# A graph layer on one core: block-first tile space, near blocks loaded up to four bands at a time, and row finishing moved from GpSimd to VectorE

## The chip, the cores and the metric

The kernel runs on one core of a Trainium2 chip, as one launch. The metric is device time in microseconds (us); the kernel before takes 1089.55 us (median of 3 runs, 1089.52 to 1090.64). Lower is better.

## The reference

`x` is 8192 x 128 and `adj` is 8192 x 8192, all float32. `adj` is 256 MiB, so reading it is the bulk of the traffic.

```python
def _L0_gnn_ref(x, adj, w):
    A = adj + jnp.eye(adj.shape[0], dtype=adj.dtype)
    deg = jnp.sum(A, axis=1)
    d_isqrt = jax.lax.rsqrt(deg)
    A_hat = A * d_isqrt[:, None] * d_isqrt[None, :]
    h = jnp.matmul(A_hat, x)
    return jax.nn.elu(jnp.matmul(h, w))
x = _layernorm(x + _L0_gnn_ref(x, adj, L0_gnn_w), axis=-1)
```

Row sums of `adj` are needed before any product that uses them: the product of a column band t of `A` with band t of `x` needs the square root of the degrees of row band t.

## The kernel before, in words

The 8192 rows and columns are cut into 16 bands of 512. Tile (t, u) is the 512 x 512 piece of `adj` in row band u and column band t, 1 MiB. SBUF holds 22 slots of 1 MiB (`SLOTS`), each either a tile or a "home", which is band t of `x` scaled by d and copied four times over quadrants for TensorE. Steps for a tile: a load on SyncE's queue; row sums on ScalarE (ACT) by a copy with `accum_out`, one instruction for each block of 128 rows; a transposition of 32 x 32 blocks on VectorE (DVE), called a turn; then a TensorE (PE) step of 64 matmuls against home t, which handles one to four tiles at once; then DVE adds the product from PSUM into `hT`. In the code a step is a "part", and a "job" is what is summed in one of the two PSUM sets (`SETS`) before one add.

A home t can be made only when row band t has been read completely, since only then is its degree known. Therefore rows are read ahead: of row t the tiles that can't be kept are read for their sums alone ("far" loads, up to 2048 columns wide) and read a second time late ("again"), and those near the diagonal are kept ("first"). The last load of row t is the diagonal tile (t, t). On it follow, in this order, ACT's sum, DVE's reduction of the sums (`deg`), on GpSimd (POOL) the addition of the identity to the diagonal tile and then the power -1/2, on DVE the scaling of `x` (line 803) and ten of the sixteen copies into the home (line 810), the other six on ACT (line 668). PE's first step on home t needs these.

When all 16 products of row band u are added, the row is finished: an "out" on PE (four matmuls with `w`), then z on ACT (scale by d, line 686), two Relu and an Exp on ACT, ELU on DVE (828), residual on POOL (639), statistics on DVE (836, 842), deviation on POOL (645, 649), shift on DVE (849), normalisation (702) and store on ACT.

The order of each engine's instructions is fixed ahead by `plan()`, a planner in Python that plays the work through with assumed durations, and the engines then run these lists with semaphores between them. Nothing is reordered while the kernel runs. `KEEP` says how many tiles may be kept over which bands, `FEED` how many loaded tiles may wait before rows are read on, `FLIGHT` how many loads the planner holds in flight, `MERGE` how many tiles one step takes. Tiles merge into one step only if their slots lie at equal distances of less than 16 (`even_slots`).

## Time and profile before

| | |
|---|---|
| median of 3 runs | 1089.55 us |
| the profiled execution | 1089.98 us |
| its span, first to last instruction | 1087.7 us |
| mean granted TensorE clock | 0.956 of full speed |
| PE busy | 929.3 us (85%) |
| DVE busy | 807.2 us (74%) |
| ACT busy | 809.3 us (74%) |
| POOL busy | 78.7 us (7%) |
| bytes moved by DMA | 363.89 MB |

The profiled execution took 2.3 us more than its span. Durations below are from it. Busy shares are averages over stages with different limits, so the rows further down are taken stage by stage. DMA queues run behind their issue: a load is issued some 13.4 us (median) before it lands.

### The profile page before, as it was taken

The numbers are of one execution on the slowest core, as the hardware profiler recorded it, in microseconds if no ns is written. First come the engines' busy times: TensorE is split into PE (matmuls) and PEld (weight loads), VectorE is DVE, ScalarE is ACT, GpSimd is POOL, SyncE is SP. The second block draws the span as 40 slices with busy tenths as digits, with TensorE's granted clock in tenths as the row PEclk, the third lists the DMA queues.
The fourth block names the chain that finished last, engine by engine and source line by source line (L and its number), as shares of the span: only waits on it lengthen the run. The fifth ranks groups of instructions, "written<-read, shape, count | busy, mean of one in ns | idle before, by whom it ended". The sixth has DMA issues, their size and how long they took to land.

```text
span 1087.7 us, 36085 instructions
## 1 busy us (share of the span) xinstructions
PE 929.3 (85%) x16128; PEld 831.2 (76%) x16128; DVE 807.2 (74%) x761; ACT 809.3 (74%) x2033; POOL 78.7 (7%) x87
## 2 busy tenths in 40 slices
PE   0089399399698988999999999999997999999993
PEld 0077289297475755998889999999896889899993
DVE  0686686694868697998789999999975765757822
ACT  6898898898899999898999999967419756200203
POOL 0000000000000000000000000010101130100101
PEclk9999799699698998999999999999998999999997
DMA  9999999999999999999999999958984979799910
GB/s 379 383 391 409 385 393 408 383 388 403 385 398 390 396 383 394 386 395 376 395 396 378 369 375 320 320 192 266 306 293 150 324 215 315 250 325 309 366 72 20
DMA packets 178506, 363.89 MB, mean 335 GB/s; under 512 B 6192, under 2 KB 34480, under 8 KB 170672
## 3 DMA queue, kind: packets, MB, share of 16 engines
q1 hardware_dynamic: 161456, 353.20, 89.4%
q10 hardware_dynamic: 16896, 8.39, 2.6%
q8 instruction: 127, 2.08, 0.8%
q14 instruction: 27, 0.22, 0.1%
HBM read 357.37 MB, written 4.19 MB: 332 GB/s over the span
## 4 chain that ended last, share of the span: by engine, by line
PE 38%; issue 24%; DMA 21%; ACT 5%; DVE 4%; SPq 4%; POOL 3%; POOLq 0%; DVEq 0%
PE p_set L772 38%; DMA tile<-in_adj 20%; ACT tile L660 4%; SPq L611 4%; DVE tile L810 2%; POOL tile L639 1%; POOL rstd L649 1%; DVE hT L821 1%; DMA xn<-in_x 1%; DVE tile L790 1%; POOL tile L628 1%; DVE xn L803 0%; POOL var_eps L645 0%; ACT tile L668 0%; PE p_set L746 0%
## 5 line engine op out<-in xcount | busy, mean ns | idle before, releaser
L772 PE MATMUL p_set<-tile 32*128 32x256 f32 (+3 forms) x16000 | 912.5, 386 | 138.6 <-DVE tile L790 59.5
L772 PEld LDWEIGHTS p_set<-tile 32*128 32x128 f32 x16000 | 815.7, 189 | 231.2 <-issue 141.9
L790 DVE STREAM_TRANSPOSE tile<-tile 128x2048 f32<-128x2048 f32 x256 | 583.5, 2297 | 161.4 <-ACT tile L660 92.2
L660 ACT ACTIVATE tile<-tile 128x512 f32<-128x512 f32 (+2 forms) x824 | 592.6, 720 | 49.4 <-DMA tile<-in_adj 44.6
L668 ACT ACTIVATE tile<-xn 32x512 f32<-32x512 f32 x208 | 130.4, 627 | 31.6 <-DVE xn L803 24.1
L660 ACT ACTIVATION_READ_ACCUMULATOR tile<-tile 128x1 f32 x824 | 153.9, 187 | 0.0
L821 DVE TENSOR_TENSOR hT<-p_set,hT 128x512 f32<-128x512 f32 (+1 forms) x137 | 109.0, 828 | 55.2 <-PE p_set L772 54.5
L686 ACT ACTIVATE tile<-p_set,d 128x128 f32<-128x128 f32 x64 | 18.2, 366 | 158.2 <-PE p_set L746 158.2
L810 DVE COPY tile<-xn 32x512 f32<-32x512 f32 x160 | 66.8, 418 | 5.0
L628 POOL TENSOR_TENSOR tile<-tile,ident 128x512 f32<-128x512 f32 x16 | 20.4, 1274 | 686.4 <-ACT tile L660 686.4
L702 ACT ACTIVATE tile<-tile,shift,rstd 128x128 f32<-128x128 f32 x64 | 26.1, 485 | 29.1 <-DVE shift L849 29.1
L639 POOL TENSOR_TENSOR tile<-tile 128x512 f32<-128x512 f32 x16 | 20.3, 1268 | 267.9 <-DVE tile L828 267.9
L803 DVE TENSOR_TENSOR xn<-xn,d 128x512 f32<-128x512 f32 x23 | 15.2, 660 | 11.8 <-DMA xn<-in_x 11.8
L746 PEld LDWEIGHTS p_set<-w_sb,hT 128*128 128x128 f32 x128 | 15.5, 191 | 10.5 <-issue 6.1
L823 DVE COPY hT<-p_set 128x1024 f32<-128x1024 f32 (+1 forms) x7 | 9.6, 1372 | 18.7 <-PE p_set L772 18.7
L746 PE MATMUL p_set<-w_sb,hT 128*128 128x128 f32 x128 | 18.5, 287 | 5.3 <-DVE hT L821 4.1
L828 DVE SCALAR_TENSOR_TENSOR tile<-tile 128x512 f32<-128x512 f32 x16 | 10.7, 669 | 8.4 <-ACT tile L696 8.4
L649 POOL TENSOR_TENSOR rstd<-var_eps,half 128x4 f32<-128x4 f32 x16 | 16.6, 1037 | 1.3
L634 POOL TENSOR_TENSOR d<-deg,half 128x4 f32<-128x4 f32 x16 | 16.3, 1020 | 4.5 <-DVE deg L796 4.3
L836 DVE BATCH_NORM_STATS2 stats<-tile 128x6 f32<-128x128 f32 x64 | 13.5, 273 | 1.6 <-POOL tile L639 1.6
L695 ACT ACTIVATE tile<-tile 128x512 f32<-128x512 f32 x16 | 10.1, 630 | 0.5
L693 ACT ACTIVATE tile<-tile 128x512 f32<-128x512 f32 x16 | 10.1, 630 | 0.4
(15 smaller groups left out, 30.8 us busy)
## 6 DMA issues: line engine op xcount, KB each, us to landing
tile<-in_adj SPq DMA_DIRECT2D x331, 1024.0 KB, 13.4
xn<-in_x SPq DMA_DIRECT2D x23, 256.0 KB, 12.0
tile<-in_x ACTq DMA_DIRECT2D x16, 256.0 KB, 7.7
out_rows<-tile ACTq DMA_DIRECT2D x16, 256.0 KB, 8.3
w_sb<-in_w SPq DMA_DIRECT2D x1, 64.0 KB, 1.9
```

Source lines behind the costliest of these rows:

```text
L611: sp.dma_start(shaped(k), source(loads[k])).then_inc(loaded[slot_of[k]], 16)
L628: nc.gpsimd.tensor_tensor(on_diagonal, on_diagonal, ident[:, :].unsqueeze(1).to_broadcast([128, BLOCKS, 128]), ALU.add)\
L639: nc.gpsimd.tensor_tensor(pos[:, n % RING], pos[:, n % RING], res[:, n % RING], ALU.add).then_inc(y_ready, 1)
L649: nc.gpsimd.tensor_tensor(rstd[:, n % RING], var_eps[:, :], half[:, :], ALU.pow).then_inc(rstd_ready, 1)
L660: ins = nc.scalar.activation(view[:, g], view[:, g], ACT.Copy, accum_out=to[:, g:g + 1])
L668: nc.scalar.activation(xs_part(h, q, s), xn[quadrant(s), h % XN], ACT.Copy).then_inc(copied_by["act"], 1)
L702: ins = nc.scalar.activation(pos[:, n % RING, b], pos[:, n % RING, b], ACT.Identity, bias=shift[:, n % RING, b:b + 1], scale=rstd[:, n % R ...
L746: ins = nc.tensor.matmul(p[:, 0, F * b:F * (b + 1)], hT[:, at:at + 128], w_sb[:, :], start=True, stop=True)
L772: ins = nc.tensor.matmul(to, xs_of(h)[quadrant(q), j], moving, start=first and s == b == 0, stop=last and s == b == 3)
L790: nc.vector.transpose(tiles[slot_of[k]], tiles[slot_of[k]]).then_inc(tile_turned, 1)
L810: nc.vector.tensor_copy(xs_part(h, q, s), xn[quadrant(s), h % XN]).then_inc(copied_by["dve"], 1)
L821: nc.vector.tensor_tensor(rows, new, rows, ALU.add).then_inc(product_added, 1)
```

## The change

The space of 22 slots is laid out with the block index first: `[128, BLOCKS, SLOTS, BAND]` instead of `[128, SLOTS, 2048]`. A tile is now four runs of 512 columns, 22 x 512 apart, and slots n and n+1 lie side by side in each block. So any two tiles may form one step, and one load can bring 2 or 4 neighbouring bands of a row: `near` loads of 4 bands x 1 block (8 KB rows) or 2 bands x 2 blocks (4 KB rows) in place of 4 or 2 tile loads with 2 KB rows. Far loads now have a ring of their own, four rows of 1 MiB in slots 0 to 3, which become ordinary slots when the last far load is summed. Constants of the planner change, and its rules (a step of m tiles isn't taken if it would leave one over). The home's copies come in three pieces, and the planner calls a home usable after the first. The diagonal addition is held back until the power if the diagonal tile completes the row. z, the positive part plus residual, ELU, statistics and the sum of variance and epsilon are on DVE; ACT keeps one Relu and the Exp, POOL the power alone.

Over the whole program the planner's lists hold these numbers, before and now: steps of 1, 2, 3, 4 tiles 11, 99, 13, 2 and 4, 112, 8, 1 (125 steps both); adjacency loads 331 and 336 (331 and 333 MiB, since 77 tiles are read again, not 75); of these `near` loads none and 30 (8 of four bands, 22 of two); row sums on ACT 824 and 744 instructions; homes 23 and 22.

```diff
-KEEP = (12, 9, 10)
+STAGE = 4
+KEEP = (12, 11, 7)
-STAY = 13
+STAY = 12
+WIDTHS = (4, 2)
-FEED = 10
-FLIGHT = 4
+FEED = 12
+FLIGHT = 5
+FIRST_COPIES = [("dve", [(0, q) for q in range(Q)]), ("act", [(2, 2), (2, 3)] + [(3, q) for q in range(Q)]),
+                ("dve", [(1, q) for q in range(Q)] + [(2, 0), (2, 1)])]
+LATE_COPIES = [("act", [(s, q) for q in range(Q)]) for s in range(Q)]
...
+    def near_loads():
+        left = [v for v in row_todo if v[0] == "near"]
+        r, slots = left[0][2], sorted(n for _, n in free)
+        for w in WIDTHS:
+            if len(left) < w or len(free) < w + 1 or left[0][1] - left[w - 1][1] != w - 1:
+                continue
+            runs = [n for n in slots if all(n + i in slots for i in range(w))]
+            if not runs:
+                continue
+            base, t0, nk = runs[0], left[w - 1][1], BLOCKS // w
...
+            return [("near", r, nk * j, nk, t0, w, base, j, group) for j in range(w)]
+        _, t, r = row_todo.pop(0)
+        return [tile_load("first", t, r)]
...
+    def tile_summed(i):
+        _, t, u, _, _ = tiles[i]
+        if t != u:
+            offer("dve", 4 if t in known else 6, "turn", i, 2.35)
+        elif sums_left[u]:
+            offer("pool", 1, "diagonal", i, 1.4)
+        else:
+            held_diagonals[u] = i
...
         elif kind == "power":
             known.add(arg)
             offer("dve", 0, "scale", home_of[arg], 0.7)
+            if arg in held_diagonals:
+                offer("pool", 1, "diagonal", held_diagonals.pop(arg), 1.4)
...
-        tile = sb("tile", [128, SLOTS, 2048])
-        tiles = [tile[:, n] for n in range(SLOTS)]
+        space = sb("space", [128, BLOCKS, SLOTS, BAND])
+        slots = [space[:, :, n] for n in range(SLOTS)]
...
+            if load[0] == "near":
+                _, _, k0, nk, _, w, base, _, _ = load
+                return space[:, k0:k0 + nk, base:base + w].rearrange("p k n c -> p k (n c)")
+            _, _, _, nk, _, wide, row = load
+            return space[:, row, 0:STAGE].rearrange("p n c -> p (n c)")[:, 0:nk * wide].rearrange("p (k c) -> p k c", k=nk)
...
-                k = arg
-                wait_vacant(sp, ("load", k))
-                sp.dma_start(shaped(k), source(loads[k])).then_inc(loaded[slot_of[k]], 16)
+                load = loads[arg]
+                if load[0] == "tile":
+                    wait_vacant(sp, ("tile", load[5]))
+                elif load[0] == "near" and not load[7]:
+                    for i in near_groups[load[8]]:
+                        wait_vacant(sp, ("tile", i))
+                elif load[0] == "far" and row_before[arg] is not None:
+                    sp.wait_ge(act_summed, sum_nth[row_before[arg]])
+                sp.dma_start(home_of(load), source(load)).then_inc(arrival(arg), 16)
...
-                            moving = bass.AP(chunk.tensor, chunk.offset, [[SLOTS * 2048, 32], [2048 * step, len(at)], [BAND, BLOCKS], [1, 32]])
+                            moving = bass.AP(chunk.tensor, chunk.offset, [[BLOCKS * SLOTS * BAND, 32], [BAND * step, len(at)], [SLOTS * BAND, BLOCKS], [1, 32]])
...
+                elif kind == "z":
...
+                    nc.vector.tensor_tensor(pos[:, n % RING], p_set[set_of_out[n]][:, 0, :].rearrange("p (b f) -> p b f", b=BLOCKS),
+                                            d[:, finals[n]].unsqueeze(2).to_broadcast([128, BLOCKS, F]), ALU.mult).then_inc(z_ready, 1)
+                elif kind == "relu":
...
+                    nc.vector.scalar_tensor_tensor(out=res[:, n % RING], in0=pos[:, n % RING], scalar=0.0, in1=res[:, n % RING],
+                                                   op0=ALU.max, op1=ALU.add).then_inc(relu_added, 1)
                 elif kind == "elu":
...
+                    nc.vector.scalar_tensor_tensor(out=pos[:, n % RING], in0=neg[:, n % RING], scalar=-1.0, in1=res[:, n % RING],
+                                                   op0=ALU.add, op1=ALU.add).then_inc(y_ready, 1)
...
+                    nc.vector.tensor_scalar(var_eps[:, n % RING], mv[:, n % RING, :, 1], EPS, None, ALU.add).then_inc(var_ready, 1)
```

VectorE, at the point where row band 8 has been read completely (`TENSOR_REDUCE deg` is its degree, line 803 or 889 the scaling, line 810 or 896 the copies into home 8, 821 or 907 adds from PSUM). Before:

```order
L790 STREAM_TRANSPOSE tile<-tile 128x2048
L796 TENSOR_REDUCE deg<-sums 128x4
L790 STREAM_TRANSPOSE tile<-tile 128x2048
L803 TENSOR_TENSOR xn<-xn,d 128x512
L810 COPY tile<-xn 32x4x128 x10
L821 TENSOR_TENSOR hT<-p_set,hT 128x4x4x32 x3
L790 STREAM_TRANSPOSE tile<-tile 128x2048 x2
L821 TENSOR_TENSOR hT<-p_set,hT 128x4x8x32
```

and now:

```order
L876 STREAM_TRANSPOSE space<-space 128x4x512
L882 TENSOR_REDUCE deg<-sums 128x4
L889 TENSOR_TENSOR xn<-xn,d 128x512
L896 COPY space<-xn 32x4x128 x10
L907 TENSOR_TENSOR hT<-p_set,hT 128x4x8x32
L876 STREAM_TRANSPOSE space<-space 128x4x512
L907 TENSOR_TENSOR hT<-p_set,hT 128x4x8x32
L876 STREAM_TRANSPOSE space<-space 128x4x512 x2
```

The turn of the diagonal tile, which stood between the degree and the scaling, now stands behind the copies. The three adds behind the copies, which free both PSUM sets, have become one; the other set's add now stands ahead of the degree.

TensorE, in the late stage, on the last seven steps of the group of rows 4 and 5 (a step is x64; 128x256 is a step of two tiles, 128x128 of one; `w_sb` is an out). Before:

```order
L746 MATMUL p_set<-w_sb,hT 128x128 x4
L772 MATMUL p_set<-tile 128x256 x64
L746 MATMUL p_set<-w_sb,hT 128x128 x4
L772 MATMUL p_set<-tile 128x128 x128
L772 MATMUL p_set<-tile 128x256 x192
L772 MATMUL p_set<-tile 128x128 x128
```

and now:

```order
L858 MATMUL p_set<-space 128x256 x64
L836 MATMUL p_set<-w_sb,hT 128x128 x4
L858 MATMUL p_set<-space 128x256 x64
L836 MATMUL p_set<-w_sb,hT 128x128 x4
L858 MATMUL p_set<-space 128x256 x256
L858 MATMUL p_set<-space 128x128 x128
```

The first pair of single tiles has become one step of two; the second pair, which uses two different homes, is still two steps.

SyncE's list of loads, from its beginning (128x4x512 is a tile, 128x2048 a far load or, now, also a load of four bands). Before:

```order
L611 DMA tile<-in_adj 128x2x1024 x2
L611 DMA tile<-in_adj 128x2048 x8
L611 DMA tile<-in_adj 128x4x512 x6
L607 DMA xn<-in_x 128x4x128
L611 DMA tile<-in_adj 128x4x512 x9
```

and now:

```order
L723 DMA space<-in_adj 128x2x1024 x2
L723 DMA space<-in_adj 128x2048 x12
L723 DMA space<-in_adj 128x2x1024 x2
L713 DMA xn<-in_x 128x4x128
L723 DMA space<-in_adj 128x4x512 x11
```

Of the twelve loads of 2048 columns eight are far and four bring bands 2 to 5; the two behind them bring bands 0 and 1. The load of `x` stands behind the same 16 MiB.

## Rows read from the trace of the kernel before

**Rows 1.** Windows: length; busy PE, PEld, DVE, ACT, POOL; PE clock; DMA share; GB/s
```profile
59.50:598.80 539.30, 470.21 (x7812) 398.54 (x7812) 422.99 (x338) 498.54 (x1291) 20.32 (x18) 0.93 1.04 392
598.80:1068.20 469.40, 456.74 (x8304) 430.65 (x8304) 355.32 (x382) 254.78 (x623) 50.05 (x54) 0.99 0.83 276
...
740.00:830.00 90.00, 83.31 (x1480) 77.84 (x1476) 72.05 (x81) 47.15 (x93) 10.48 (x12) 0.96 0.81 264
...
1068.20:1087.70 19.50, 2.30 (x18) 1.94 (x16) 6.38 (x21) 9.02 (x22) 5.37 (x6) 0.65 0.09 27
```
**Rows 2.** Waits from 100 to 600 us: total us, times, longest
```profile
PE p_set L772 <- DVE tile L810: 57.6, 5, 18.7
```
**Rows 3.** Timeline around the last load of row 8: start us, length us
```profile
547.04 0.63 ACT L660 ACTIVATE tile<-tile 128x512 f32<-128x512 f32 x1
...
550.72 0.18 DVE L796 TENSOR_REDUCE deg<-sums 128x4 f32<-128x68 f32 x1
550.99 2.31 DVE L790 STREAM_TRANSPOSE tile<-tile 128x2048 f32<-128x2048 f32 x1
553.23 0.65 DVE L803 TENSOR_TENSOR xn<-xn,d 128x512 f32<-128x512 f32 x1
553.91 4.45 DVE L810 COPY tile<-xn 32x512 f32<-32x512 f32 x10
558.39 1.89 DVE L821 TENSOR_TENSOR hT<-p_set,hT 128x512 f32<-128x512 f32 x3
...
559.74 2.64 PE L772 MATMUL p_set<-tile 32*128 32x256 f32 x41 [2.70 <-DVE hT L821]
```
**Rows 4.** The same around the last load of row 7
```profile
504.04 0.63 ACT L660 ACTIVATE tile<-tile 128x512 f32<-128x512 f32 x1
...
507.91 1.01 POOL L634 TENSOR_TENSOR d<-deg,half 128x4 f32<-128x4 f32 x1
...
512.81 2.54 PE L772 MATMUL p_set<-tile 32*128 32x256 f32 x32 [2.28 <-DVE tile L810]
```
**Rows 5.** Windows with far loads alone, and with tile loads
```profile
9.00:31.00 22.00, 0.00 (x0) 0.00 (x0) 0.00 (x0) 18.79 (x22) 0.00 (x0) 1.00 1.01 416
56.00:85.00 29.00, 25.55 (x420) 23.87 (x424) 25.52 (x15) 28.58 (x85) 0.00 (x0) 1.00 1.05 390
```
**Rows 6.** PE's timeline: steps of two tiles, then of one tile
```profile
783.50 21.00 PE L772 MATMUL p_set<-tile 32*128 32x256 f32 x384
...
882.63 4.97 PE L772 MATMUL p_set<-tile 32*128 32x128 f32 x168
890.02 6.31 PE L772 MATMUL p_set<-tile 32*128 32x128 f32 x128 [2.42 <-issue]
```
**Rows 7.** Timeline of the end, after the last step
```profile
1068.28 1.22 DVE L821 TENSOR_TENSOR hT<-p_set,hT 128x1024 f32<-128x1024 f32 x1 [26.24 <-PE p_set L772]
...
1079.02 1.26 POOL L639 TENSOR_TENSOR tile<-tile 128x512 f32<-128x512 f32 x1
...
1083.27 1.65 ACT L702 ACTIVATE tile<-tile,shift,rstd 128x128 f32<-128x128 f32 x4 [1.28 <-DVE shift L849]
```
**Rows 8.** Groups by form: count, busy us, mean ns
```profile
L821 DVE TENSOR_TENSOR hT<-p_set,hT 128x512 f32<-128x512 f32 x102 | 64.6, 673 | 21.8 <-PE p_set L772 21.6
L772 PE MATMUL p_set<-tile 32*128 32x128 f32 x1408 | 43.5, 277 | 2.7 <-issue 2.7
```
**Rows 9.** PE's waits for adds from 598.8 to 1068.2 us
```profile
PE p_set L772 <- DVE hT L821: 6.1, 4, 3.2
...
PE p_set L746 <- DVE hT L821: 2.6, 1, 2.6
```
**Rows 10.** Timeline: far loads summed one after the other by ACT
```profile
16.28 1.91 ACT L660 ACTIVATE tile<-tile 128x2048 f32<-128x2048 f32 x1 [0.48 <-DMA tile<-in_adj]
...
18.77 1.91 ACT L660 ACTIVATE tile<-tile 128x2048 f32<-128x2048 f32 x1 [0.49 <-DMA tile<-in_adj]
```
**Rows 11.** The page's part 6, DMA issues: KB each, us to landing
```profile
tile<-in_adj SPq DMA_DIRECT2D x331, 1024.0 KB, 13.4
...
w_sb<-in_w SPq DMA_DIRECT2D x1, 64.0 KB, 1.9
```

More of the change, by code:

```diff
@@ L111, in allowed @@
         if kind == "out":
-            return free_set() is not None and len(late) == LATE and counts["outs"] == counts["z"]
+            return free_set() is not None and counts["residuals"] > 0 and counts["outs"] == counts["z"]
         if kind == "z":
@@ new lines, in next_load @@
+        if pick_row:
+            pick_row = bool(free_rows) if row_todo[0][0] == "far" else len(free) >= 2
+        if firsts and free and (backlog < FEED or not pick_row):
+            t, u = firsts.pop(0)
+            return tile_load("first", t, u)
+        if pick_row:
+            if row_todo[0][0] == "far":
+                row = min(free_rows)
+                free_rows.remove(row)
+                return row_todo.pop(0) + (row[1],)
+            queued.extend(near_loads())
+            return queued.pop(0)
@@ L409, in plan @@
     assert len(finals) == BANDS and counts["stored"] == BANDS
-    return loads, slot_of, homes, tenants, late, jobs, parts, finals, order, turns, (now, busy, dma)
+    return loads, tiles, homes, tenants, late, jobs, parts, finals, order, turns, (now, busy, dma)
 def gcn_resnorm(nc: bass.Bass, x: bass.AP, adj: bass.AP, w: bass.AP, out: bass.AP):
@@ L417, in gcn_resnorm @@
     AX = mybir.AxisListType
-    loads, slot_of, homes, tenants, late, jobs, parts, finals, order, turns, _ = plan()
+    loads, tiles, homes, tenants, late, jobs, parts, finals, order, turns, _ = plan()
     def nth_of(engine, kind):
@@ new lines, in signal_of @@
+    def signal_of(load):
+        if load[0] == "far":
+            return ("row", load[6])
+        return ("slot", load[4]) if load[0] == "tile" else ("slot", load[6] + load[7])
+    near_groups = {}
+    for i, (_, _, _, _, some) in enumerate(tiles):
+        if loads[some[0]][0] == "near":
+            near_groups.setdefault(loads[some[0]][8], []).append(i)
+    arrived, counts = [], {}
+    for load in loads:
+        counts[signal_of(load)] = counts.get(signal_of(load), 0) + 16
+        arrived.append(counts[signal_of(load)])
@@ new lines, in arrival, with sums_of, xs_chunk @@
+        def arrival(k):
+            kind, n = signal_of(loads[k])
+            return (row_loaded if kind == "row" else loaded)[n]
+        def sums_of(load):
+            if load[0] == "tile":
+                _, _, t, u, _, _ = load
+                return sums[:, BLOCKS * u:BLOCKS * (u + 1), t]
+            _, r, k0, nk, at, _ = load[:6]
+            return sums[:, BLOCKS * r + k0:BLOCKS * r + k0 + nk, at // BAND if load[0] == "far" else at]
+        def xs_chunk(h, j):
+            return slots[homes[h][1]][:, j // Q, F * (j % Q):F * (j % Q + 1)]
@@ L579, in wait_vacant @@
                 engine.wait_ge(part_out, last_part[arg] + 1)
-            elif loads[arg][0] == "far":
-                engine.wait_ge(act_summed, sum_nth[arg])
+            elif what == "stage":
+                engine.wait_ge(act_summed, max(sum_nth[k] for k in row_before))
             else:
@@ L748, in _ @@
                     continue
-                job, h, ks, first, last = parts[arg]
+                job, h, these, first, last = parts[arg]
                 bank, rows, _ = jobs[job]
```

484 lines of the change are left out of this document (246 added, 238 removed).

## The prediction

> **What bounds the kernel now.** I read the windows first. The profiled execution has three parts [rows 1]. From 59.5 to 598.8 us the DMA share is full (1.04, 392 GB/s) and PE is busy only 470.2 of 539.3 us: reading bounds. From 598.8 to 1068.2 us PE is busy 456.7 of 469.4 us at a clock of 0.99 while DMA has fallen to 276 GB/s: PE bounds. The last 19.5 us are a chain for the two last rows. DVE and ACT are busier than 70% on the whole, but neither is the limit in either stage.
>
> Next the waits tell what PE lacks in the first stage: 57.6 us in 5 waits for copies into a home [rows 2]. A home needs the degree of its row band, and this needs the last load of the row. So the first stage is a chain of restarts, one for each band: last load of row t lands, ACT sums it, DVE and POOL make d, DVE scales and copies, PE starts. Then PE has a fixed stock of work, since each band opens the same tiles whatever the planner does. I counted this in both lists of loads: row 7 ends after 185.75 MiB, row 8 after 202.00 and row 9 after 216.25, before and now, and when PE begins with bands 7, 8 and 9 it has 148, 136 and 125 of the 256 tiles left, before and now. Only the last restart before PE is full counts; a gain at an earlier one is waited away at the next. The last two with idle time worth naming are at 512.8 us (band 7, 2.28 us waited) and 559.7 (band 8, 2.70 waited) [rows 3, 4]. After that PE waits 8.7 us for adds and hardly at all for anything else [rows 1, 9].
>
> **Part 1: loads of two and four bands.** Far loads with 8 KB rows ran at 416 GB/s, tile loads with 2 KB rows at 390 [rows 5]: 2.52 against 2.69 us for a MiB, 0.17 us less. Up to the end of row 8 the new order brings 8 MiB in loads of four bands (8 x 0.17 = 1.4 us) and 14 MiB in loads of two, with 4 KB rows that no row here prices; between 0 and 0.17 I take the middle (14 x 0.085 = 1.2 us). Term: -2.6 us, from 0 to -3.7. All of it is on the path while reading bounds.
>
> The Trainium skill speaks against this term: "DMA: Bandwidth & Descriptors", section Specifications, asks for transfers of at least 512 B for line rate, so rows of 2 KB would run as fast as rows of 8 KB. By this rule the term would be 0 and the sum 2.6 us higher. The trace does not agree, by its 416 against 390 GB/s.
>
> **Part 2: the way from a row's last load to PE's first step.** At band 8 it took 559.74 - 547.04 = 12.7 us [rows 3]: ACT's sum (four times the 0.63), the degree at 550.72 (behind a turn), the turn of the diagonal tile until 553.2, scaling 0.65, ten copies 4.45, then adds from 558.39, of which the first two must free a PSUM set before PE may start. In the new list the diagonal turn stands behind the copies, and the add that frees the set stands ahead of the degree. What is left: degree done at 550.9, power 1.01 [rows 4], scaling 0.65, four of ten copies 1.8, some 0.2 for hand-overs: 554.6. That is only when the home is ready; PE must also have finished band 7. There the diagonal turn is replaced by another turn between degree and scaling, so only the copies shorten: power done at 508.9, turn until 509.2, scaling and four copies 2.45, so PE starts at 511.8 in place of 512.8. Its twelve tiles are now six steps of two, 21.00 / 3 = 7.0 us each [rows 6], with 1 us for a first step that catches up with the copies: 511.8 + 43 = 554.8. So band 8 starts at 554.8, not 559.7. Term: -4.9 us, from 0 (other work on DVE gets in between) to -6. It adds to part 1, since both move the restart. What is late next is nothing until band 9: 11 tiles are five steps of 7.0 and one of 43.5 / 11 = 3.95 [rows 8], 38.95 us, before 39.1.
>
> **Part 3: fewer single tiles in the PE-bound stage.** Two single tiles in a row cost more than a step of two: from 882.63 to 890.02 + 6.31 = 896.33 there are 296 records, 40 of them of the next step (40/128 x 7.0 = 2.2 us), so two singles took 11.5 us [rows 6]. They are one step of 7.0 now. Term: -4.5 us. The second such pair stays, one more single is gone for a triple (under 1 us, from 0). Steps of three and four in place of two I price at 0: they have the same columns to stream, and those in question are few (13 and 2 before, 8 and 1 now).
>
> **Part 4: the end.** Before, POOL's residual of the last row, 1.26 us, stands in the chain at 1079.02, late by the first row's work on POOL [rows 7], and so do a second Relu of ACT and z in four instructions. New chain from 1068.28: add to 1069.5, out to 1070.8, z on DVE priced as the add of 512 columns, 0.67 [rows 8], then the second out 71.6 to 72.7 and z to 73.5; the first row's ELU and statistics hold DVE until 75.7, the second row's (Relu and residual and ELU at 0.67 each, estimated 1.5 for statistics and variance) until 78.5; power 79.6, shift 79.8, and ACT's normalisation waits for the first row's until 80.4, so 82.1. Before, normalisation ended at 1083.27 + 1.65 = 1084.9. One more store issue of 0.4 stands behind it. Term: -2.4 us, from 0 to -4.
>
> **Part 5: what is added.** z, Relu with residual and the variance sum put about 0.67 + 0.67 + 0.2 us on DVE for each of 16 rows, 25 us in all, nearly all in the PE-bound stage, where DVE is busy 355 of 469 us [rows 1]. z stands on DVE behind PE's out, and an engine that waits there holds back all turns behind it. In this stage PE waits 6.1 and 2.6 us for adds [rows 9] and only 12.7 us in all (469.4 - 456.7, rows 1), so hardly for a turn: the turns have a lead that covers this; if the cover is gone, PE pays up to the DVE time of the dense part, 7 rows x 1.54 = 11 us. A PSUM set is now freed by DVE in its turn, and behind a turn of 2.3 us; the new list again has a single-set collision behind the rows 8 and 9. Term: +1.5 us, from -1 to +11. ACT loses 80 sum instructions and POOL its row work; neither is on the path, so 0. The two further MiB of reading fall in the late stage (DMA share 0.83), so 0. Block-first turns, copies and matmul operands have the same element counts; strides are larger, and no row shows that case. I take 0, because the old home copies already wrote four pieces 2 KB apart and took 4.45 / 10 = 0.45 us each; with 256 turns a 1% slower turn would be 6 us of DVE and only partly on the path.
>
> **Sum.** 1089.98 - 2.6 - 4.9 - 4.5 - 2.4 + 1.5 = 1077.1 us against the profiled execution, 2.3 of it outside the span. That execution was 0.4 us above the median of the runs, so 1076.7; I say 1077.
>
> **The rivals.**
>
> *The ring of far loads starves the queue (slower).* SyncE may issue a far load only when the one four before it has been summed, and everything behind it waits too, tile loads and `x` included. Loads land every 2.49 us there [rows 10], so four take 10.0 us; the sum needs 1.9 and a little more, the transfer 2.5, and issue to landing of a small load takes 1.9 [rows 11]: some 3.5 us are left for ACT to be late. ACT is busy 498.5 of 539.3 us in this stage [rows 1], and its six copies into a home come in one piece. Against it: the queue is deep (13.4 us from issue to landing, rows 11), and tile loads between far loads stretch the ring. Some 62 far loads to the end of row 8 reuse a row; from 12.9 / 62 = 0.2 us lost at each, the whole gain is gone. At 0.4 us each it is 25 us: 1077 + 25 = 1102. Chance 0.08.
>
> *DVE becomes the bound where rows are finished.* From 740 to 830 us DVE is busy 72.05 of 90 us [rows 1]; seven rows add 11, which is 92%, before any wait for PE's outs. For it: waits in program order. Against it: rows 9. It gives back about 8 us: 1085. Chance 0.17.
>
> *Reading is not earlier.* Groups of two or four bands need adjacent slots that are all vacated, their tiles are turned only when every load of the group is summed, and 18 slots serve tiles where 22 did. Parts 1 and 2 then come to nothing: 1077 + 7.5 = 1084. The row at 550.72, late by a turn, speaks for it, since the new lists have turns there too. Chance 0.13.
>
> *More than forecast.* With shorter idle times the clock stays up (0.93 in the first stage, rows 1), and the 8.7 us that PE waits for adds in the second [rows 9] go too: 1077 - 8 = 1069. Chance 0.15.
>
> **How the numbers follow.** The forecast has 0.47, the ring 0.08, DVE 0.17, reading 0.13, more 0.15. The bounds of the terms, joined, go from about 1067 to 1088; this also takes in the DVE and reading cases and half of the last. It leaves out the ring and the other half of the last, 0.15 together. The likeliest case alone is 1072 to 1081. A measurement can't tell less than 0.2% from no change, 2.2 us: faster is below 1087.4. The forecast, the better case and nearly all of DVE and reading are there: 0.88. Same 0.04, from the ends of these two. Slower 0.08, the ring.
>
> **What would show it.** Part 1: over 395 GB/s up to the start of band 8. Part 2: not over 8.5 us from the landing of row 8's last load to the first step of band 8, and PE's long full stretch begins at 590 to 593 us, where 125 tiles are left. Part 3: only three steps of 128 columns behind it, and 462 to 467 us from there to the last step. Part 4: 17 us from the last step to the end. Part 5: no wait of PE for turns in the late stage, and z rows of about 0.67 us. The forecast is wrong if DMA falls below 385 GB/s in the first stage (ring), if PE waits for line 876 after 740 us (DVE), or if turns take over 2.35 us each.

## The result and the profile after

The changed kernel takes 1085.2 us (median of 5 runs, 1083.96 to 1086.72) against 1089.55 before (now of 5 runs, 1088.8 to 1091.97); the ratio is 0.9951, with a 95% interval of 0.9931 to 0.9972. It is faster, by some 4 to 5 us where 12.5 were forecast. The time is inside the range of 1067 to 1088, above the likeliest case's own 1072 to 1081. The profiled execution took 1086.72 us, its span 1084.9.

I cut the span of after where I cut it before [rows 1]: at the step with 125 tiles left and at the end of the last step. Two windows are added for what follows.

```profile
core 0: us, PE busy (x) PEld busy (x) DVE busy (x) ACT busy (x) POOL busy (x), PEclk, DMA share, GB/s
59.50:599.70 540.20, 469.81 (x8066) 434.58 (x8066) 428.14 (x307) 486.00 (x1203) 20.45 (x18) 0.94 1.02 386
599.70:1068.10 468.40, 457.15 (x8048) 415.12 (x8048) 376.44 (x418) 221.96 (x492) 27.71 (x26) 0.99 0.85 285
1068.10:1084.90 16.80, 2.33 (x20) 1.94 (x16) 8.27 (x27) 5.70 (x12) 2.39 (x2) 0.67 0.11 31
910.00:1062.00 152.00, 143.60 (x2572) 132.34 (x2568) 104.86 (x93) 23.22 (x43) 4.03 (x4) 0.99 0.82 275
340.00:600.00 260.00, 240.08 (x4228) 228.01 (x4232) 219.78 (x168) 233.37 (x600) 12.84 (x12) 0.96 1.00 374
```

The last two windows in the kernel before:

```profile
340.00:600.00 260.00, 240.78 (x4040) 200.77 (x4036) 221.28 (x191) 243.39 (x649) 13.60 (x12) 0.97 1.04 389
910.00:1062.00 152.00, 150.14 (x2830) 141.06 (x2826) 96.75 (x80) 25.71 (x57) 10.13 (x12) 1.00 0.81 274
```

The stage that reading bounds is not shorter but 0.9 us longer, and from 340 to 600 us it reads at 374 in place of 389 GB/s with a DMA share of 1.00 in place of 1.04. And PE, which before was busy 150.1 of 152 us near the end, is busy 143.6. Both losses are in stretches where the forecast had a gain or nothing. The stations below are worked out from the traces of the profiled executions (us; "125 left" and "40 left" are the starts of the first step with so many tiles to go; row 8 and 9 are the landings of these rows' last loads):

```
                                 row 8   row 9   125 left  40 left  last step ends  span
before                           547.0   586.1   598.8     922.5    1068.2          1087.7
after                            548.5   591.0   599.7     913.8    1068.1          1084.9
slots given back (e1)            546.9   590.2   598.3     914.7    1058.5          1075.8
before, slots kept back (e2)     546.7   585.9   600.3     925.1    1077.6          1097.1
no near loads (e3)               551.2   592.5   603.6     921.8    1076.3          1093.2
rows as before (e4)              548.9   590.4   598.8     915.5    1067.4          1087.0
after, half products (e5)        540.5   578.4   587.4     878.7    1008.0          1024.7
before, half products (e6)       544.4   582.9   595.6     878.0     997.5          1017.0
e1, restart undone (e7)          565.6   612.5   625.3     954.3    1098.9          1115.6
e1, five steps split (e8)        549.3   589.8   598.3     932.8    1076.4          1093.1
before, restart as after (e9)    546.6   585.8   595.3     925.1    1072.8          1092.3
e1, other constants (e10)        547.8   586.5   595.1     904.3    1049.2          1065.5
```

So after against before: +0.9 to 125 left, -9.6 from there to 40 left, +8.6 over the last 40 tiles (154.3 in place of 145.7), -2.7 behind the last step: -2.8 us of span.

Who waits in the first stage: SyncE's waits from 340 to 640 us, first of after, then of before (total, times, longest).

```profile
SPq L723 <- PE p_set L858: 152.3, 34, 9.3
SPq L691 <- PE p_set L858: 19.0, 3, 6.5
SPq L723 <- ACT space L764: 6.0, 6, 3.4
```

```profile
SPq L611 <- PE p_set L772: 67.1, 25, 6.2
SPq L611 <- ACT tile L660: 42.7, 21, 5.8
```

The ring of far loads is not what it waits for (ACT's 6.0 us). It waits for PE to give back slots of tiles, 171.3 us (both lines of PE) in place of 67.1, and before row 7's and row 9's groups of near loads nothing lands for 6.1 and 5.6 us. The plans fit this: by `kept_units()` 11 and 10 tiles are kept over rows 8 and 9 in the kernel before, of 22 slots, and 12 and 12 in the changed one, of 18.

The waits of PE and then of DVE in after, from 910 to 1062 us:

```profile
PE p_set L858 <- DVE space L876: 6.9, 6, 2.0
PE p_set L858 <- issue: 1.4, 1, 1.4
```

```profile
DVE space L876 <- DMA space<-in_adj: 36.5, 27, 3.7
```

PE waits for turns and the turns for loads, though the DMA share is only 0.82. The loads come too late because they have few slots: the 20 tiles of rows 2 and 3, with which the last 40 begin, go through 5 slots (9, 16, 17, 18, 21), before through 9. The code says why: `close_stage()`, which gives the ring's slots 0 to 3 to tiles, is called only behind the sum of a far load, and the last far load is summed before `rows_done` is set. So they are never given back, though the description of the change has them become ordinary slots.

The page's rows for turns and for z:

```profile
L876 DVE STREAM_TRANSPOSE space<-space 128x2048 f32<-128x2048 f32 x256 | 580.1, 2292 | 113.0 <-ACT space L764 64.3
L918 DVE TENSOR_TENSOR space<-p_set,d 128x512 f32<-128x512 f32 x16 | 10.8, 676 | 5.6 <-PE p_set L836 5.6
```

The larger strides cost nothing (2292 ns a turn, 2297 before), and z takes 0.68 us, as priced.

### The profile page after: what moved, and what is told of

Read it like the earlier page. It is cut to its first block, busy times and chain, and to the rows that moved or that the text cites. A ratio compares the mean times of both kernels' runs of the same rounds, so it can differ in the third digit from the quotient of the medians.

```text
span 1084.9 us, 35847 instructions
## 1 busy us (share of the span) xinstructions
PE 929.3 (86%) x16128; PEld 851.6 (79%) x16128; DVE 832.0 (77%) x770; ACT 759.0 (70%) x1777; POOL 53.6 (5%) x55
## 4 chain that ended last, share of the span: by engine, by line
PE 59%; DMA 16%; DVE 11%; ACT 7%; issue 4%; SPq 2%; POOL 0%; DVEq 0%; ACTq 0%
PE p_set L858 58%; DMA space<-in_adj 15%; ACT space L764 5%; DVE space L876 5%; DVE space L896 2%; SPq L723 2%; DVE hT L907 1%; DVE xn L889 1%; ACT space L772 1%; PE p_set L836 1%; DMA xn<-in_x 1%; DVE stats L936 1%; DVE space L930 0%; ACT space L795 0%; POOL d L748 0%
## 5 line engine op out<-in xcount | busy, mean ns | idle before, releaser
L858 PE MATMUL p_set<-space 32*128 32x256 f32 (+3 forms) x16000 | 912.5, 385 | 141.1 <-DVE space L876 88.1
L858 PEld LDWEIGHTS p_set<-space 32*128 32x128 f32 x16000 | 836.2, 188 | 213.6 <-issue 146.2
L876 DVE STREAM_TRANSPOSE space<-space 128x2048 f32<-128x2048 f32 x256 | 580.1, 2292 | 113.0 <-ACT space L764 64.3
L764 ACT ACTIVATE space<-space 128x512 f32<-128x512 f32 (+2 forms) x744 | 577.8, 778 | 70.1 <-DMA space<-in_adj 66.2
L907 DVE TENSOR_TENSOR hT<-p_set,hT 128x1024 f32<-128x1024 f32 (+2 forms) x100 | 106.3, 1077 | 81.7 <-PE p_set L858 81.3
L772 ACT ACTIVATE space<-xn 32x512 f32<-32x512 f32 x192 | 120.3, 627 | 45.7 <-DVE xn L889 36.8
L764 ACT ACTIVATION_READ_ACCUMULATOR space<-space 128x1 f32 x744 | 138.8, 187 | 0.0
L896 DVE COPY space<-xn 32x512 f32<-32x512 f32 x160 | 66.8, 417 | 5.0
L795 ACT ACTIVATE space<-space,shift,rstd 128x128 f32<-128x128 f32 x64 | 26.2, 481 | 27.5 <-DVE shift L951 27.4
L930 DVE SCALAR_TENSOR_TENSOR space<-space 128x512 f32<-128x512 f32 x16 | 10.7, 670 | 2.7 <-ACT space L789 2.6
L924 DVE SCALAR_TENSOR_TENSOR space<-space 128x512 f32<-128x512 f32 x16 | 11.1, 692 | 0.3
```

The costliest lines, as they stand in the source:

```text
L764: ins = nc.scalar.activation(view[:, g], view[:, g], ACT.Copy, accum_out=to[:, g:g + 1])
L772: nc.scalar.activation(xs_part(h, q, s), xn[quadrant(s), h % XN], ACT.Copy).then_inc(copied_by["act"], 1)
L795: ins = nc.scalar.activation(pos[:, n % RING, b], pos[:, n % RING, b], ACT.Identity, bias=shift[:, n % RING, b:b + 1], scale=rstd[:, n % R ...
L858: ins = nc.tensor.matmul(to, xs_chunk(h, j)[quadrant(q)], moving, start=first and s == b == 0, stop=last and s == b == 3)
L876: nc.vector.transpose(slots[slot], slots[slot]).then_inc(tile_turned, 1)
L896: nc.vector.tensor_copy(xs_part(h, q, s), xn[quadrant(s), h % XN]).then_inc(copied_by["dve"], 1)
```

## The experiments

Ratios are to the kernel before, run between on the same chip, with the 95% interval in brackets. In the code, `...` stands for lines left out.

**Late stage.** e1 gives the four slots back; e2 takes four slots from the kernel before.

```diff
                 else:
                     rows_done = True
+                    close_stage()
```

> The changed kernel with one line more: when the last row has been read, the four slots of the far ring are given back to the tiles. In the changed kernel as it is, the test for this stands only behind the sum of a far load, the last far load is summed while rows 12 to 15 are still to be read, and so the slots are never given back: the tiles of rows 2 and 3 are read again through 5 slots, before through 9. Theory A (stranded slots): PE's last 40 tiles take 145 to 146 us, as before, not 154.3 (913.8 to 1068.1), DMA lands the second readings 10 us and more ahead of PE, and the time is 1085.2 - 8 = 1077 (1075 to 1079). Rival B (PE-bound anyway: the row work now on DVE takes the turns' time): PE still waits for turns and the time stays at 1084 to 1086.

Measured: 1077.62 us, ratio 0.9879 (0.9852 to 0.9906). The last 40 tiles take 143.8 us.

```diff
+        elif rows_done and len(stranded) < 4:
+            stranded.append(slot)
         else:
             free.append((now, slot))
...
-    pending_x = []
+    pending_x, stranded = [], []
```

> The kernel before with nothing changed but four slots that are not given back once all rows are read, so that the tiles of rows 2 and 3 are read again through 5 slots. Theory A: the loss that the changed kernel shows appears here as well, without any of its other changes: 4 to 9 us more, 1094 to 1098, all of it after 910 us. Rival B (the slots don't matter, DVE does): no change, 1088.5 to 1090.5.

Measured: 1099.71 us, ratio 1.0081 (1.0055 to 1.0107). That is above the 1094 to 1098 expected. The last 40 tiles take 152.5 us in place of 145.7. So the four slots are worth 10.5 us in the changed kernel and 6.8 in the one before, over these tiles. With the slots back, PE's waits from 910 to 1062 us are these, none of them for a turn:

```profile
PE p_set L837 <- DVE hT L908: 1.4, 1, 1.4
PE p_set L859 <- issue: 0.9, 1, 0.9
PE p_set L837 <- DVE space L919: 0.8, 1, 0.8
```

**First stage.** e3 loads every tile alone.

```diff
-WIDTHS = (4, 2)
+WIDTHS = ()
```

> The changed kernel without loads of two and four bands (WIDTHS empty): near tiles come one by one, and the planner makes its lists anew. It is about the first stage. There row 4 lands 2.5 us earlier than before and row 9 4.9 us later (591.0 against 586.1). Theory C (a group of adjacent slots has to be vacant as a whole, so the queue runs dry: gaps of 6.1 and 5.6 us before the groups of rows 7 and 9): row 9 lands by 586 to 588 and PE's full stretch begins at about 596. Rival D (18 slots are too few, grouped or not): row 9 lands at 590 or later, since the narrow loads lose another 3 us. The whole time moves little in both cases, since four slots are still stranded: 1083 to 1090.

Measured: 1096.83 us, ratio 1.0062 (1.0041 to 1.0083). That is above the 1083 to 1090 expected. Without groups row 9 lands still later, and the rate from 340 to 600 us stays at 375 GB/s. That the grouping dries the queue falls: the shortage comes with the ring, its 18 slots for tiles and the new constants, with groups or without. The groups are worth 8 us of span in the profiled executions and 12 us by the two ratios.

e5 and e6 leave out half of each product (blocks 1 and 2 of each tile), in after and in before, so that PE gives slots back early. This is the cut that tells the wait for slots from all else in the order of loads.

```diff
-                    for b in range(BLOCKS):
+                    for b in (0, 3):
                         j = Q * b + s
```

> The changed kernel with half of each product left out: PE multiplies blocks 0 and 3 of each tile and not blocks 1 and 2, so a step of two takes some 3.5 us in place of 7.0 and slots are given back at once; list of loads, copies and turns as they are. Theory S (in the first stage tiles have 18 slots in place of 22, so loads wait for PE to give slots back): with slots free early the loads no longer wait, the last load of row 9 lands in the changed kernel earlier than in the kernel before under the same cut, by the 2.6 us forecast for loads of two and four bands (0 to 3.7), and the DMA rate in 60 to 500 us is over 395 GB/s. Rival Q (the order of the list, the ring of four rows or ACT's sums hold the queue, with PE or without): row 9 stays 4 to 5 us later than in the kernel before under the same cut.

> The kernel before with the same half of each product left out, for comparison with the changed kernel so cut. Theory S: row 9 lands 0 to 4 us later than there. Rival Q: row 9 lands 4 to 5 us earlier than there, as uncut (586.1 against 591.0 us). In both theories row 9 lands here no later than uncut, 586 us, and by at most some us earlier, since reading bounds the stage.

Measured: 1027.5 and 1019.1 us (two runs each). From 340 to 600 us, e5 and then e6:

```profile
340.00:600.00 260.00, 154.13 (x2240) 127.56 (x2240) 228.14 (x175) 243.72 (x622) 11.32 (x10) 0.84 1.04 392
```

```profile
340.00:600.00 260.00, 156.21 (x2024) 119.30 (x2028) 221.82 (x191) 246.38 (x659) 12.45 (x12) 0.78 1.04 390
```

SyncE's wait for PE from 340 to 640 us, 171.3 us in after, is 65.8 us in e5:

```profile
SPq L723 <- PE p_set L858: 55.4, 29, 5.4
SPq L691 <- PE p_set L858: 10.4, 2, 6.0
```

With slots free early the changed list reads at full share. Row 8 lands 3.9 us and row 9 4.5 us before the other kernel's, and the 125-left step starts 8.2 us before (587.4 against 595.6), where parts 1 and 2 had -7.5. So both parts together do what was forecast and a little more, and in the whole kernel the wait for slots takes it all back. (Behind 125 left e5 is slower than e6: it has the four slots that are never given back.)

The loads of these traces give the price of each width directly. From one landing to the next behind a load of the same kind it takes, up to 600 us and in the median, 2.71 us in before for a tile (2 KB rows, 113 times), and in after 2.58 us for a load of two bands (4 KB, 10 times) and 2.48 us for one of four (8 KB, 6 times; far loads 2.50). The 14 and 8 MiB up to the end of row 8 make 14 x 0.13 + 8 x 0.23 = 3.7 us, near the 3.9 measured. The Trainium skill ("DMA: Bandwidth & Descriptors", section Specifications) asks for 512 B for line rate, by which rows of 4 and 8 KB would read no faster than 2 KB; these times and the 3.9 us of row 8 say otherwise.

e7 undoes part 2 in e1, without a new plan: it moves instructions of the finished lists. It also goes further: PE waits for all copies of a home before a step on it, where before and after it waits for each quarter of the copies as it comes to it.

```diff
+    own = {tiles[i][1]: i for i in range(len(tiles)) if tiles[i][1] == tiles[i][2]}
+    for t in range(BANDS):
+        h = min(h for h in range(len(homes)) if homes[h][0] == t)
+        dve, pool = order["dve"], order["pool"]
+        dve.remove(("turn", own[t]))
+        dve.insert(dve.index(("scale", h)), ("turn", own[t]))
+        dve.remove(("copies", (h, 2)))
+        dve.insert(dve.index(("copies", (h, 0))) + 1, ("copies", (h, 2)))
+        if pool.index(("diagonal", own[t])) > pool.index(("power", t)):
+            pool.remove(("diagonal", own[t]))
+            pool.insert(pool.index(("power", t)), ("diagonal", own[t]))
...
-                    for engine, many in sorted(max(copied[h, (s, q)] for q in range(Q) if copied[h, (s, q)][0] == e)
-                                               for e in {copied[h, (s, q)][0] for q in range(Q)}):
+                    for engine, many in copied_last[h].items():
```

> The changed kernel with its slots given back, and part 2 undone in the same plan: the diagonal tile is turned ahead of the scaling of its band, the ten copies of DVE stand in one piece, and PE waits for all sixteen copies of a home before a step. Theory of the forecast (the restart is on the path): band 8 begins 4 to 5 us later behind the landing of its row than with the slots given back (12.7 in place of 8.8 us), PE's full stretch begins 4 to 5 us later than 598.3, and the kernel takes 1082 us in place of 1077.6. Rival (the loads that wait for slots set the restart, and the way behind the landing is slack): under 1.5 us, 1078 to 1079; or more than 5, since slots given back later also delay the next rows: 1084 and more.

Measured: 1121.91 us, ratio 1.0299 (1.0266 to 1.0332), far above the 1082 of the forecast's theory and on the side of the rival's "more than 5". Band 8 begins 12.9 us behind its row in place of 8.9, as before the change (12.7). But at bands 2, 3, 4 and 7 it is 11.6 to 13.8 us, where the kernel before has 8.8. Band 2 shows the further edit, the copies and PE's first step, in e7 and then in before:

```profile
208.94 4.45 DVE L907 COPY space<-xn 32x512 f32<-32x512 f32 x10
213.65 3.68 PE L869 MATMUL p_set<-space 32*128 32x256 f32 x36 [15.53 <-DVE space L907]
```

```profile
209.23 4.46 DVE L810 COPY tile<-xn 32x512 f32<-32x512 f32 x10
211.14 3.37 PE L772 MATMUL p_set<-tile 32*128 32x256 f32 x28 [18.65 <-DVE tile L810]
```

So e7 does not price part 2. What it shows is how delays add up with few slots: each of the nine restarts from band 1 to 9 is 2.1 to 6.4 us longer than in e1, 39.0 us in sum, and row 5 lands 8.2, row 7 14.0 and row 9 22.3 us later; the full stretch begins 27.0 us later. The delay of each band is passed on to later rows' landings, since loads wait for the slots of that band.

e9 is the counterpart: part 2 alone in the kernel before, again in its finished lists.

```diff
...
+        if dve[at + 1][0] == "add":
+            dve.insert(dve.index(("scale", h)), dve.pop(at + 1))
+        dve.remove(("turn", own[t]))
+        dve.insert(dve.index(("copies", h)) + 1, ("turn", own[t]))
+        pool.remove(("diagonal", own[t]))
+        pool.insert(pool.index(("power", t)) + 1, ("diagonal", own[t]))
```

> The kernel before (22 shared slots) with part 2 alone, in its own plan: at each band the diagonal tile is turned and its addition done behind the copies and the power, and the add that frees a PSUM set stands ahead of the scaling. Nothing else moves. Theory of the forecast: the way from the landing of row 8's last load to band 8's first step falls from 12.7 to about 9 us, PE's full stretch begins 4 to 5 us earlier than 598.8, and the kernel takes 1085 us. Theory M (each restart counts, since slots come back earlier at each band and the next row is read earlier; in the changed layout undoing part 2 moved the full stretch by 27 us): more than 6 us, 1083 or less. Rival N (with 22 slots reading is full anyway, and the next row's landing is fixed): 0 to 3 us, 1087 to 1090.

Measured: 1096.77 us, ratio 1.0055 (1.0033 to 1.0078). With 22 slots the rows land as before (546.6, 585.8), and 125 left comes 3.5 us earlier, near the forecast. Band 8's restart took 9.9 us and not 9, because the add that was moved ahead of the scaling waited 2.33 us for PE there. Then the gain is lost: from 125 to 40 left it takes 329.8 us in place of 323.7, and the last 40 tiles 2.0 us more. DVE, in the kernel before from 600 to 740 us:

```profile
600.00:740.00 140.00, 139.92 (x2464) 133.80 (x2460) 135.03 (x144) 124.07 (x360) 13.60 (x12) 1.00 0.89 305
```

It has 5 us to spare there. The diagonal turn does not go away but stands behind the copies, and in e9 the second step of band 9 waits 2.25 us for an add behind three turns. That step then takes 8.7 us in place of 6.9, at a granted clock of 0.80 behind the idle time. The step in e9 and then in before:

```profile
605.20:613.90 8.70, 8.69 (x128) 8.00 (x132) 8.70 (x6) 8.70 (x29) 0.00 (x0) 0.80 1.04 378
```

```profile
605.80:612.70 6.90, 6.90 (x133) 6.90 (x129) 6.90 (x6) 6.90 (x23) 0.00 (x0) 1.00 1.05 382
```

The wait and the clock are 4.1 us, more than the 3.5 gained. The rest is made of smaller differences, and no step from 595 to 1070 us waits for a turn. So all of M's, N's and the forecast's times fell; of the forecast only the restart itself (9.9 us behind the landing, 3.5 us earlier) came out roughly.

**Singles.** e8 does five steps of two (68, 70, 72, 78, 80) as ten singles, in e1.

```diff
...
+        if n in SPLIT:
+            split += [(job, h, these[:1], first, last), (job, h, these[1:], first, last)]
...
```

> The changed kernel with its slots given back, and five steps of two in the PE-bound stage (steps 68, 70, 72, 78 and 80 of the plan) done as two single tiles each, in the same PSUM set, all else in the same order. Theory of the forecast (two singles in a row cost 11.5 us against 7.0): 4.5 us each, 22 us in all, 1100 us in place of 1077.6. Rival (most of the 11.5 us was the step that came behind and its wait): under 2 us each, 1088 or less.

Measured: 1095.45 us, ratio 1.0052 (1.0032 to 1.0073). From 125 to 40 left it takes 334.5 us in place of 316.4: 18.1 / 5 = 3.6 us for each pair, between the 4.5 of the forecast and the rival's 2. But two single steps as such are hardly slower than one of two: the pair at 675.65 us, where PE does not stop, takes 7.15 us, and the step of two in e1 6.91. What costs is that PE stands still more often, for reasons that the profile doesn't name ("issue"), and that the granted clock then falls. PE's waits at "issue" from 598 us to 40 left in e8 and in e1, and two windows of e8, the pair without a stop and another pair with one of 3.16 us:

```profile
PE p_set L870 <- issue: 14.1, 8, 3.2
```

```profile
PE p_set L859 <- issue: 1.6, 3, 0.9
```

```profile
675.65:682.80 7.15, 7.15 (x264) 7.15 (x259) 7.00 (x8) 7.08 (x22) 0.00 (x0) 1.00 0.80 291
655.00:669.00 14.00, 10.79 (x270) 10.41 (x266) 5.63 (x3) 5.22 (x18) 0.00 (x0) 0.76 0.48 156
```

So 3.6 us is a mean over places that differ: from the start of a pair to the next step it is 0.2 to 6.8 us more than in e1. What PE waits for at "issue" stays open.

**Rows on DVE.** e4 finishes rows as the kernel before does (z and both Relus on ACT, residual and variance on POOL).

```diff
...
-            offer("dve", 1, "z", arg, 0.95)
+            offer("act", 1, "z", arg, 1.25)
...
-            offer("pool", 0, "deviation", arg, 1.15)
+            offer("pool", 1, "residual", arg, 1.4)
...
```

> The changed kernel with the rows finished as before (z and two Relu on ACT, residual and variance on POOL), planned anew; all else stays. What I forecast for this part alone: the end after the last step is 2.4 us longer (19.2 to 19.6 us against 16.8), and DVE has 25 us less to do in the late stage, which is worth at most 1.5 us to PE: 1086 to 1088. Rival (DVE is the limit in the late stage): PE's waits for turns go down, and the time falls to 1082 or less in spite of the longer end.

Measured: 1088.62 us, ratio 0.9978 (0.9959 to 0.9997). The last step ends at 1067.4, as in after, and what stands behind it takes 19.6 in place of 16.8 us.

**A better version.** e10 is e1 with other constants and far loads of part width priced by their bytes in the plan; e11 is e1 again.

```diff
-KEEP = (12, 11, 7)
+KEEP = (12, 7, 9)
...
-STAY = 12
+STAY = 10
...
-MERGE = 4
+MERGE = 3
...
-FLIGHT = 5
+FLIGHT = 4
...
```

> The changed kernel with its slots given back and other constants of the plan: KEEP (12, 7, 9), STAY 10, MERGE 3, FLIGHT 4, and far loads of part width priced by their bytes in the plan. Fewer tiles of the early rows are kept, so more are read again late and fewer hold a slot in the first stage. Theory S (slots bound the first stage): row 9 lands earlier than 590 us and PE's full stretch begins before 598, in all 1068 to 1075 us. Rival (the plan's picture of the first stage is off by more than these constants give): 1076 to 1082, no better than with the slots given back alone.

> The changed kernel with its slots given back, once more and on the same chip as the two others, as their base: 1077 to 1078 us.

Measured: 1067.41 us, ratio 0.9781 (0.9757 to 0.9805), and for e11 1076.47 us, 0.9873 (0.9846 to 0.9900). Row 9 lands at 586.5, as in the kernel before, and 125 left is at 595.1, though there are still the ring and 18 slots. Over rows 8 and 9 this plan keeps 9 tiles each in place of 12, and SyncE's waits for PE from 340 to 640 us are 114.3 us in place of e1's 171.2. So the 18 slots alone do not make the shortage; they do so with what the plan keeps in them. The constants and the price of far loads changed together, so that the kept tiles do it is not shown.

**The restart's missing microsecond.** In after, band 8's restart (DVE, POOL, PE):

```profile
552.22 0.18 DVE L882 TENSOR_REDUCE deg<-sums 128x4 f32<-128x68 f32 x1
552.49 1.02 POOL L748 TENSOR_TENSOR d<-deg,half 128x4 f32<-128x4 f32 x1 [43.12 <-DVE deg L882]
553.48 1.29 POOL L742 TENSOR_TENSOR space<-space,ident 128x512 f32<-128x512 f32 x1
553.54 1.78 DVE L889 TENSOR_TENSOR xn<-xn,d 128x512 f32<-128x512 f32 x1 [1.13 <-POOL d L748]
...
555.35 4.45 DVE L896 COPY space<-xn 32x512 f32<-32x512 f32 x10
...
557.26 4.99 PE L858 MATMUL p_set<-space 32*128 32x256 f32 x56 [2.35 <-DVE space L896]
```

The scaling takes 1.78 us, with POOL's held addition beside it. e12 (on e10) and e13 (on e1) make that addition wait for the scaling; e14 is e10 again.

```diff
+                    t = tiles[i][1]
+                    if order["pool"].index(("power", t)) < order["pool"].index(("diagonal", i)):
+                        pool.wait_ge(x_scaled, min(scale_nth[h] for h in range(len(homes)) if homes[h][0] == t))
```

> The kernel with the other constants, and POOL's diagonal addition of a band waits until DVE has scaled that band's x. In the changed kernel the scaling took 1.76 us where this addition of 1.29 us ran beside it on POOL (553.48 beside 553.54) and 0.65 us alone in the kernel before. Theory P (the two slow each other, and the restart pays): the scalings of the bands take 0.65 to 0.75 us throughout, each restart comes up to 1.1 us earlier, and since slots then come back earlier at every band, PE's full stretch begins 2 to 5 us earlier than 595.1; in all 1062 to 1066 us. Rival (the scaling is slow for another reason, or the 1.1 us is waited away): scalings still at 1.7 us, or the full stretch within 1 us of 595.1 and the time within 1.5 us of the base.

> The changed kernel with its slots given back and the same wait of POOL's diagonal addition for the scaling. Theory P: full stretch 2 to 5 us earlier than 598.3 to 599.2, 1071 to 1075 us in place of 1076.5 to 1077.6. Rival: 1076 to 1078.

> The kernel with the other constants once more, as the base of the one whose addition waits: 1067.4 us.

Measured: e12 1070.21 us, ratio 0.9817 (0.9790 to 0.9844); e14 1066.79, 0.9777 (0.9751 to 0.9803); e13 1082.82, 0.9925 (0.9901 to 0.9950). In e13's band 8:

```profile
556.63 1.02 POOL L752 TENSOR_TENSOR d<-deg,half 128x4 f32<-128x4 f32 x1 [43.45 <-DVE deg L886]
...
557.68 0.69 DVE L893 TENSOR_TENSOR xn<-xn,d 128x512 f32<-128x512 f32 x1 [1.13 <-POOL d L752]
...
558.41 5.41 DVE L900 COPY space<-xn 32x512 f32<-32x512 f32 x10
...
558.52 1.43 POOL L746 TENSOR_TENSOR space<-space,ident 128x512 f32<-128x512 f32 x1 [0.87 <-DVE xn L893]
```

The scaling is short again (0.65 to 0.69 in all bands), so it was the addition beside it. But now the addition falls beside the copies, which take 5.41 in place of 4.45 us, all of it in the second of the ten (1.38 in place of 0.42 us). The time from the degree to PE's first step stays as it was (5.0 and 4.9 us). Theory P was right on the cause and wrong on the gain. Why both kernels are slower, by 3 to 6 us, is not settled; in e13 the degree also came later, behind an add and a turn (row 8 lands at 551.8, degree at 556.37).

## Why the prediction was wrong, point by point

**What failed.** In the first stage it is a step of the first part: "All of it is on the path while reading bounds." I had the landings as MiB divided by a rate, to which SyncE's waits for slots do not belong. At every band from 2 to 9 the way from landing to first step is shorter than before, and still row 8 lands 1.5 and row 9 4.9 us later, where 2.6 us earlier was forecast. With slots free early (e5, e6) row 8 lands 3.9 us earlier. With this step falls the sentence that only the last restart counts, since "a gain at an earlier one is waited away at the next". It holds where rows land at their own pace: in the kernel before (e9: no landing of rows 5 to 9 moved by more than 0.8 us). In the changed kernel a load waits for a slot, the slot for a step, and the step for the restart, so each row's landing hangs on the bands before it (e7: restarts 39.0 us longer in sum moved row 9 by 22.3). The shortage is of slots beside those that the plan keeps occupied; no run has the changed layout with 22 slots, so how much is the ring's and how much the constants' isn't shown.

The rival "Reading is not earlier" named the 18 slots and gave 1084; it had 0.13. It was right to 125 left, for that reason and not for the turns that I gave as its evidence. That its 1084 is so near to 1085.2 is luck: behind 125 left it took over the forecast's terms, of which the largest was too small by 5.1 us and another, put at 0, was 8.6.

**Part 1** was right in kind and low: -3.9 us at row 8 with slots free (e5, e6), forecast -2.6, and just outside its own bound of -3.7. Rows of 8 KB saved 0.23 us for a MiB and not 0.17, and those of 4 KB, at 0.13, lie near the middle that I took. **Part 2** was 8.8 us from landing to first step, not 7.6, and nearly all of the difference is the scaling, 1.78 us for 0.65. I had moved the addition beside it at no cost. Together they gave -8.2 with slots free, forecast -7.5, and +0.9 in the kernel as it is.

**The end of the reading** was put at nothing: "The two further MiB of reading fall in the late stage (DMA share 0.83), so 0". The term that is missing there is the four slots: the last 40 tiles took 8.6 us longer than before, and 10.5 us longer than with the slots back (e1). The DMA was not busy, but the slots were: a mean share tells nothing of how many loads may be under way. The code that gives the ring back is part of the change; I had counted its slots as given back.

**Part 3** measured -3.6 per pair for -4.5 (e8), and its reason fell: without a stop of PE two singles take 7.15 us, a step of two 6.91. The 11.5 us that the part took for two singles had a stop of 2.42 us in it, and from 886.3 to 894.0 us, over this stop and the second single, the granted clock was 0.78. The stretch gained 9.6 us in all, twice the forecast: PE's idle time in it fell from 11.1 to 4.2 us, its waits for adds alone from 8.7 [rows 9] to 2.4. With -1.0 in place of -3.0 from 125 left to the last step, the late stage as a whole comes near the forecast only because two misses, -5.1 and +8.6, stand against each other.

**Part 4** was right: 16.8 us behind the last step, forecast 17, and 19.6 in e4, without this part. **Part 5** left no trace: PE waits for a turn (line 876) only where DVE itself waits for loads, z is 0.68 us, and e4, without this work on DVE, reaches 40 left no sooner (915.5 against 913.8). So the rival "DVE becomes the bound" falls, and its condition in the prediction (a wait for line 876 after 740 us) was met by another cause. The ring starves nothing: SyncE waits 6.0 us for ACT there, 42.7 before. "More than forecast" came true in one of its two terms, the waits for adds; e10's 1067 us is another kernel and doesn't bear on it.

Measured, in spans: first stage +0.9, to 40 left -9.6, last 40 tiles +8.6, end -2.7, in all -2.8; forecast -7.5, -4.5, 0, -2.4 and +1.5 for DVE. Of the signs that the prediction named, part 1's rate up to band 8 was 390 GB/s and not over 395 (396 in e5), part 2's full stretch began at 599.7 and not at 590 to 593, and from there to the last step it took 468.4 and not 462 to 467 us; part 3's three steps of one tile and part 4's 17 us came.

## What to carry to other kernels

Where buffers are shared between streams, an earlier landing must be followed through the buffers: ask for each load whose slot it takes and who frees it, and split one pool in two only with both halves' waits counted. If SyncE waits for the consumer, the load rate is a result and not an input, and a longer restart is paid again at band after band (e7). To tell such a wait from all other causes, halve the consumer's work and leave the order alone. And before a slow step is called dear, take the idle time and the granted clock out of it.

## What the runs showed of the hardware

A DVE scaling of 128x512 took 0.65 us alone and 1.75 to 1.78 us where a POOL addition of 1.26 to 1.29 us had begun 0.06 us before it. The two did not merely slow each other: in after and in e1, at all 16 bands, the scaling ended 0.55 us behind the end of the addition, whether the addition had begun 0.06 or 1.07 us before it. The Trainium skill ("SBUF — State Buffer", section Who interferes with whom) says so: a DVE instruction with two inputs in SBUF and a POOL one that reads SBUF exclude each other. The copies have one input, and still one of the ten, the second, took 0.96 us longer beside the same addition, which itself took 1.43 us there.

Loads of 1 MiB landed every 2.71 us with rows of 2 KB, every 2.58 with 4 KB and every 2.48 to 2.50 with 8 KB (medians).

Turns of four pieces of 512 columns that lie 44 KB apart took 2292 ns, those of a contiguous tile 2297.

Two steps of one tile took 7.15 us, one step of two tiles 6.91. A step of two behind an idle time of 2.25 us took 8.7 us at a granted clock of 0.80.
